# Scales of the first layer spread through DRAM, the halves of q and k exchanged by ScalarE, and fewer transposes in front of two stages

## What is computed

```python
x = x + L0_attn(layernorm(x))           # everything below is L0_attn
x = x + einsum('btd,ed->bte', conv3(x), w_pw)      # three taps over time, then pointwise
q, k, v = split(x @ w_qkv.T)            # 16 heads of 8
q, k = rope(q, sin, cos), rope(k, sin, cos)
q_phi, k_phi = elu(q) + 1, elu(k) + 1
attn = causal_linear_attention(q_phi, k_phi, v) / (denominator + 1e-6)
x = x + sigmoid(delta(x) @ w_gate.T + b_gate) * (attn @ w_o.T)
h = layernorm(x) * ln_g + ln_b
x = x + sum_e softmax(h @ w_moe_gate.T)[e] * (silu(h @ w1[e] + b1[e]) @ w2[e] + b2[e])
```

## Time and profile before

| | us |
|---|---|
| median of three runs | 1480.37 (1479.02 to 1481.9) |
| the profiled execution's own time | 1480.5 |
| its span, first to last instruction | 1478.7 |
| setup, until the second stage starts | 8.1 |
| attention_front | 8.1 to 454.1 |
| mixture | 454.1 to about 896 |
| the three stages behind | about 900 to 1478.7 |

### The profile page before, as it was taken

How to read it: one execution, slowest core, us unless ns; L and a number is a source line. 1 busy time by engine, 2 the same in 40 slices (tenths; PEclk the granted TensorE clock), 3 DMA queues, 4 the chain that set the end, 5 groups by cost and what they waited for, 6 DMA issues and landing times. The chain is left out here.

```text
span 1478.7 us, 33273 instructions
## 1 busy us (share of the span) xinstructions
PE 1266.4 (86%) x10164; PEld 984.0 (67%) x10164; DVE 1013.0 (69%) x3390; ACT 814.8 (55%) x1703; POOL 712.6 (48%) x907
## 2 busy tenths in 40 slices
PE   2899999999986999999999965883988888739998
PEld 1566767676655877777777754773666666539997
DVE  3588888888735899999999984764566666522222
ACT  2355555556426776767777643552556555525554
POOL 3355565656420234343443542335566676426666
PEclk9799999999877999999999986996999999859999
DMA  1101011110102321212112205674111112168872
GB/s 62 40 30 39 31 33 33 31 37 28 45 13 62 69 54 44 64 41 62 40 48 59 73 16 142 196 202 146 27 44 47 49 55 44 44 233 300 266 264 69
DMA packets 70844, 117.53 MB, mean 79 GB/s; under 512 B 9746, under 2 KB 36635, under 8 KB 70768
## 3 DMA queue, kind: packets, MB, share of 16 engines
q1 hardware_dynamic: 58736, 93.49, 21.3%
q0 software_dynamic: 9856, 21.52, 4.6%
q10 hardware_dynamic: 2176, 1.61, 0.4%
HBM read 79.35 MB, written 29.88 MB: 74 GB/s over the span
## 5 line engine op out<-in xcount | busy, mean ns | idle before, releaser
L1159 DVE TENSOR_TENSOR m_Sl<-m_S,m_Sh 128x512 fp32r<-128x512 f32 x256 | 195.5, 769 | 23.3 <-ACT m_S L1076 20.6
L1076 ACT ACTIVATE m_S<-PS,W 128x512 f32<-128x512 f32 x256 | 174.7, 690 | 39.0 <-issue 33.1
L1071 ACT ACTIVATE m_Sh<-PS,W 128x512 fp32r<-128x512 f32 x192 | 132.9, 692 | 72.1 <-PE PS L996 64.5
L1459 POOL DMA_INDIRECT rows<-r_row,r_posi x128 | 131.2, 1025 | 36.2 <-issue 36.0
L761 DVE TENSOR_TENSOR am<-PS,C 128x512 f32<-128x512 f32 x192 | 119.6, 678 | 25.9 <-PE PS L454 25.4
L1693 PEld LDWEIGHTS PS<-f_wt,f_hid 128*128 128x128 f32 x960 | 121.3, 194 | 4.4
L1693 PE MATMUL PS<-f_wt,f_hid 128*128 128x128 f32 x960 | 121.5, 277 | 0.0
L1682 PE MATMUL PS<-f_xT,f_wt 128*128 128x256 f32 x480 | 121.2, 390 | 0.0
L965 POOL TENSOR_TENSOR m_oe<-m_oe 128x512 f32<-128x512 f32 x48 | 67.8, 1412 | 102.2 <-DVE m_oe L1140 101.7
L994 PE MATMUL PS<-m_HH,m_w1h 128*128 128x512 f32 x256 | 107.7, 421 | 7.1 <-DVE m_w1l L1112 4.7
L352 POOL TENSOR_TENSOR am<-am,C 128x512 f32<-128x512 f32 x64 | 81.6, 1275 | 54.8 <-ACT am L636 53.5
(11 more groups left out here) (237 smaller groups left out, 3127.2 us busy)
## 6 DMA issues: line engine op xcount, KB each, us to landing
f_wt<-wr SPq DMA_DIRECT2D x40, 578.0 KB
f_row<-rows SPq DMA_DIRECT2D x40, 260.0 KB
f_wt<-wr SPq DMA_DIRECT2D x40, 256.0 KB, 2.8
m_gb<-gates SPq DMA_DIRECT2D x8, 1024.0 KB, 7.7
m_raw<-gates SPq DMA_DIRECT2D x8, 1024.0 KB, 7.9
f_row<-rows SPq DMA_DIRECT2D x40, 132.0 KB, 2.1
mid<-f_res SPq DMA_DIRECT2D x20, 256.0 KB, 3.3
X<-x SPq DMA_DIRECT2D x16, 256.0 KB, 2.8
```

What stands on the lines that cost most here:

```text
L1071: nc.scalar.activation(Sh[:, n % 4, :], PS[:, n % 3, :], ACT.Silu, bias=w("b1")[:, n:n + 1]).then_inc(sh_ready, 1)
L1076: nc.scalar.activation(S[:, n % 3, :], PS[:, n % 3, :], ACT.Silu, bias=w("b1")[:, n:n + 1]).then_inc(s_ready, 1)
L1159: nc.vector.tensor_tensor(Sl[:, n % 4, :], S[:, n % 3, :], Sh[:, n % 4, :].bitcast(F32), ALU.subtract).then_inc(sl_ready, 1)
L1459: nc.gpsimd.indirect_dma_start(out=self.rows, out_offset=bass.IndirectOffsetOnAxis(ap=self.posi[:, u, t:t + 1], axis=0), in_=self.row[:, u ...
```

## The change

- **Setup merged**: the stage `setup` is gone. Its loads and its VectorE work (`prepare`) are part of `attention_front`; SP loads x of batch 0 first of all, ScalarE's queue loads the weights, and the memset of `vm` on GpSimd comes after the first batch's scaling.
- **x comes in twice**: as tokens (into H, which is free then, for the statistics) and transposed (`xt`, an input laid out on the host: into X and, for the current batch, into `xnT`). X now holds x with features on the partitions during the front and most of the mixture. The mean is taken out by the weights (`centre`: the taps and router 0 are multiplied by I - 1/128 once). The reciprocal deviations go to DRAM and come back broadcast to all partitions (`spread_rstd`, SP), and GpSimd multiplies `xnT` by them (`scale_x`). `normalise`, `turn_xn` and `copy_xnT` are gone.
- **Denominators**: one transpose of `den` (`turn_den`), a small copy, a DMA to DRAM and a broadcast back on ScalarE's queue, in place of `spread_out`, four transposes and `copy_rdT`.
- **Second layer norm**: scale and shift go through DRAM in the same way; GpSimd does `scale_z` and `shift_z` one step later (a fifth batch e = c-1 in the pipeline); `turn_z` and `normalise2` are left for the last batch only.
- **Rotation**: ScalarE copies each half across (`swap_halves`, two instructions for q and two for k), VectorE multiplies by the sines in one operation of 128 partitions.
- **Copies**: `keep_x1` goes from GpSimd to ScalarE; ScalarE also copies x2 (`keep_x2`). `residual2` adds x2T to X from SBUF.
- **mixture**: `ROUNDED = ()`, so ScalarE makes every `Sh`. GpSimd adds X's columns to the total (`sums`, one more large addition and one small one per batch), the transposed total is the new x, ScalarE copies it into X (`copy_back`), the scores come from the total's columns right behind `back` (`pe_scores_columns`) and are multiplied by the reciprocal deviation afterwards. `residual`, `pe_turn` and the copy of xT are gone for layer 0.

The core of the diff:

```diff
@@ attention_front, SP @@
+                sp.dma_start(columns(H, b).rearrange("p (c d) -> p c d", c=CT), src).then_inc(x_in, 16)
+                sp.dma_start(columns(XT, b), xt[:, bass.ds(b * SEQ, SEQ)]).then_inc(xt_in, 16)
+            def load_rows(b):
+                after_previous(sp, pw_psum, b)
+                sp.dma_start(xnT[:, 2:], xt[:, bass.ds(b * SEQ, SEQ)]).then_inc(xnT_in, 16)
+            def spread_rstd(b):
+                sp.wait_ge(rstd1_ready, b + 1)
+                after_previous(sp, rb_in, b, 16)
+                sp.dma_start(rstd_dram.rearrange("(p t) -> p t", p=P), rstd[:, :]).then_inc(rstd_out, 16)
+                sp.wait_ge(rstd_out, 16 * b + 16)
+                after_previous(sp, xn_ready, b)
+                sp.dma_start(rb[:, :], rstd_dram.unsqueeze(0).to_broadcast([P, SEQ])).then_inc(rb_in, 16)
@@ GpSimd @@
+            def scale_x(b):
+                pool.wait_ge(rb_in, 16 * b + 16)
+                pool.wait_ge(xnT_in, 16 * b + 16)
+                nc.gpsimd.tensor_tensor(xnT[:, 2:], xnT[:, 2:], rb[:, :], ALU.mult).then_inc(xn_ready, 1)
+            def scale_z(b):
+                pool.wait_ge(x2_copied, b + 1)
+                pool.wait_ge(sb2_in, 16 * b + 16)
+                nc.gpsimd.tensor_tensor(x2c[:, :], x2c[:, :], sb2[:, 0, :], ALU.mult).then_inc(scaled, 1)
+            def shift_z(b):
+                pool.wait_ge(scaled, b + 1)
+                nc.gpsimd.tensor_tensor(x2c[:, :], x2c[:, :], sb2[:, 1, :], ALU.add).then_inc(z_ready, 1)
...
                 if b is not None:
                     mask_last(b, 0)
-                    keep_x1(b, u)
+                if e_ is not None:
+                    scale_z(e_)
+                if n is not None:
+                    scale_x(n)
...
+                if b is not None:
                     mask_last(b, 1)
+                if e_ is not None:
+                    shift_z(e_)
@@ TensorE @@
-                if n is not None:
-                    turn_xn(n)
                 if c_ is not None:
                     turn_x2(c_)
                 if b is not None:
                     update_state(b, u, 1)
+                    turn_den(b)
                     weigh(b, u, 1)
...
-                if c_ is not None:
-                    turn_z(c_)
                 if n is not None:
                     project(n, u, "q", 0)
-                if c_ is not None:
-                    logits(c_)
+                if e_ is not None:
+                    logits(e_, c_)
...
                 if b is not None:
                     weigh(b, u, 3)
-                    turn_spread(b)
@@ ScalarE @@
+            def swap_halves(b, n):
+                act.wait_ge(qk_psum, 2 * b + n + 1)
+                after_previous(act, phi_ready, b, 2)
+                for o in range(2):
+                    at, to = slice(64 * o, 64 * o + 64), slice(64 - 64 * o, 128 - 64 * o)
+                    ins = nc.scalar.activation(rot[to, n, 1, :], PS[at, 1 - n, :], ACT.Copy)
+                ins.then_inc(swapped, 1)
...
+                if f is not None:
+                    swap_halves(f, 1)
                 if b is not None:
                     copy_k(b)
...
                 if b is not None:
                     raw_scores(b, 1)
+                    keep_x1(b, u)
+                    copy_den(b)
+                    spread_den_out(b)
+                if e_ is not None:
+                    scale_h(e_)
+                if c_ is not None and not final(c_):
+                    keep_x2(c_)
                 if b is not None:
                     raw_scores(b, 2)
+                    spread_den_in(b)
+                if c_ is not None and not final(c_):
+                    spread_scale2_out(c_)
                 if n is not None:
                     copy_x1(n, u)
+                if c_ is not None and not final(c_):
+                    spread_scale2_in(c_)
                 if b is not None:
                     raw_scores(b, 3)
+                if n is not None:
+                    swap_halves(n, 0)
+                if e_ is not None:
+                    copy_logits(e_, c_)
@@ VectorE @@
-                dve.wait_ge(qk_psum, 2 * b + n + 1)
+                dve.wait_ge(swapped, 2 * b + n + 1)
                 nc.vector.tensor_tensor(rot[:, n, 0, :], PS[:, 1 - n, :], c("cos"), ALU.mult)
-                for o in range(2):
-                    at, to = slice(64 * o, 64 * o + 64), slice(64 - 64 * o, 128 - 64 * o)
-                    ins = nc.vector.tensor_tensor(rot[to, n, 1, :], PS[at, 1 - n, :], c("sin")[at], ALU.mult)
-                ins.then_inc(qk_read, 1)
+                nc.vector.tensor_tensor(rot[:, n, 1, :], rot[:, n, 1, :], c("sin"), ALU.mult).then_inc(qk_read, 1)
...
+                nc.vector.tensor_tensor(columns(XT, b), columns(XT, b), x2T[:, :], ALU.add).then_inc(x_added, 1)
@@ mixture @@
-        ROUNDED = (3,)
+        ROUNDED = ()
...
+                if e == 1:
+                    pool.wait_ge(oe_ready, MOE * b + 1)
+                    nc.gpsimd.tensor_tensor(carrier[:, :], minus_half[:, :], minus_half[:, :], ALU.mult).then_inc(carried, 1)
+                    nc.gpsimd.tensor_tensor(acc, acc, XT[:, bass.ds(b * SEQ, SEQ)], ALU.add).then_inc(with_x, 1)
+                    pool.wait_ge(with_x, b + 1)
...
                 mm.then_inc(back_psum, 1)
+                routing.pe_scores_columns(pe, b, oe[:, total_of(v), :])
...
-                    if n == 0:
-                        route(routing.pe_turn, pe, r, v, tr)
-                    if n == 3:
-                        route(routing.pe_scores, pe, r, v, tr)
...
+                    if n == 8 and p is not None:
+                        copy_back(p)
...
-                    if n == 8 and p is not None:
-                        residual(p)
```

378 lines of the change are left out of this document (208 added, 170 removed).

## The result

The changed kernel takes 1505.19 us (median of four runs, 1498.92 to 1511.71), the kernel before beside it 1481.13: ratio 1.016, 95% interval 1.011 to 1.022. It is slower by some 24 us; the prediction was 1454, with 1434 to 1479 as its range, and 0.13 on slower. The profiled execution took 1498.92, its span is 1497.1, 18.4 more than before. It is the shortest of the four, so the trace holds 18 of the 24 us.

What follows compares the result with a forecast made beforehand. In front and mixture TensorE was taken as close to full with VectorE close behind. 1480.5 - 4 (start) + 1.4 (front) - 21 + 1 (mixture) - 3.8 (end) = 1454 us, range 1434 to 1479.

Steps and rivals of the forecast that it cites:

- The start: Before the front: x loaded first and memset later, against a centring matmul and two DMA trips; -4 us, bounds -6 and 0.
- The front: Attention front: TensorE's savings offset by VectorE's waits for GpSimd; step 24.0, +0.1, about 14 steps, +1.4 us in all.
- TensorE waits there in place of the transposes: Front, before the second tile's scores: VectorE's later masks delay them 0.9 us, replacing the first 0.9 of TensorE's saving.
- so that 0.65 becomes idle time: Front: z's transposes, 0.65 us per step, stood where the next projection waits for VectorE's mask anyway, so not counted as gain.
- a further width of either sign: TensorE's granted clock, mean 0.96: less TensorE work may make low-clock stretches longer or fewer; no size given.
- Rival (a): Front: GpSimd's shared port decides, VectorE's five SBUF-only operations each wait 0.45 longer; step 26.2, 1485 us; chance 0.14.
- Rival (d): Front: ScalarE waits for a DRAM store with the last tile's raw scores behind; 1 us per step, 1468; chance 0.12.
- Rival (b): Front: waits for GpSimd fall into VectorE's gaps; step near 22.8, 1437 us; chance 0.2.
- The mixture: TensorE's transposes and VectorE's roundings and residual addition removed; -1.6 us per batch, -21 over 13, first batch +1.
- The end: End of mixture: VectorE's idle 3.77 us before the last batch's scores disappears; -3.8 us.

Runs made afterwards that it cites:

- e11: Changed kernel with GpSimd's three new front operations (scaling of x, scaling and shift of z) cut to 8 of 512 columns; 1468.90 us, 0.995 of the kernel before.
- e2: Changed kernel with four unused transposes of the identity ahead of the state update of tile 1; 1472.11 us, 0.998 of the kernel before.
- e16: Changed kernel with only the older batch's logits moved ahead of the projection of q; 1443.21 us, 0.996 of the kernel before.
- e13: Kernel before with three unused VectorE multiplications, all ahead of the denominators; 1553.78 us, 1.054 of the kernel before.
- e14: Kernel before with three unused VectorE multiplications, spread over three gaps of VectorE; 1474.62 us, 1.001 of the kernel before.
- e5: e2 with ScalarE's load of z's scales issued behind the last tile's raw scores and the copies of q's halves; 1466.05 us, 0.993 of the kernel before.
- e8: Kernel before with `ROUNDED = ()` alone, so ScalarE makes all high parts in the mixture; 1462.19 us, 0.990 of the kernel before.
- e9: e5 with the older batch's logits issued ahead of the projection of q; 1458.05 us, 0.987 of the kernel before.
- e15: Changed kernel, no filler, with the logits ahead of the projection of q and the load of z's scales later; 1466.45 us, 0.993 of the kernel before.
- e7: Kernel before with four unused transposes as filler behind the denominators of each step; 1470.68 us, 0.997 of the kernel before.
- e10: e9 with GpSimd's addition of x in the mixture moved ahead of its inverse deviation; 1452.15 us, 0.987 of the kernel before.
- e12: Kernel before with ScalarE's copies of the halves (new rotation) and no rounding on VectorE; 1459.84 us, 0.989 of the kernel before.

## Why the prediction was wrong, point by point

**The start** was right: -3.8 measured, -4 predicted; the first pointwise matmul begins at 15.76 instead of 18.91.

**The front** is the step that failed: "I take a step of 24.0, +0.1"; the steady step is 27.3. Its placing of the waits held: they are where it put them, and smaller. `x2T<-x2T,x1c` was to lose 0.5 and lost 0.36; `phi` of k 1.1, and it was 0.90; the sine of k 0.6, and it was 0.30. For the first two the overlap was foreseen within a tenth (0.50 and 1.04 us); but VectorE needs only 0.54 or 0.55 us more once GpSimd's operation has ended, and not the 0.68 that it takes alone, so 0.14 less is lost than the overlap is long. The masks of tile 1 were to begin at 10.9 after the step's start and do at 9.99 (265.91 - 255.92). The scores of tile 2 were to begin "near 13.0" and do at 12.90, but that is luck: the masks were 0.9 early, and the low clock used that up (weighing 1.94 us where it takes 1.08 at the full clock).

The Trainium skill says of the shared port that it is an exclusive lock: an instruction of VectorE with two inputs in SBUF and one of GpSimd that reads SBUF keep each other out, the one that comes second waiting (page "SBUF — State Buffer", section "Who interferes with whom"). These rows agree, and e11 takes the waits away with the GpSimd work. What I had drawn from it for the sine multiplication of q doesn't come: it takes 0.68 at 282.07 while GpSimd's power of four elements runs (281.85 to 282.86); there the measurement decides.

What the sum did not contain is what idle places of TensorE do to its clock. I had written down the idle time itself ("TensorE waits there in place of the transposes", "so that 0.65 becomes idle time"), priced each at its own length, and put the clock in one sentence as "a further width of either sign". The transposes taken out stood in exactly the two places where TensorE would otherwise wait for VectorE. Behind the first, work at the low clock then took 3.8 us longer: 0.9 each for weighing and scores, 2.1 for the pointwise matmuls. 3.4 per steady step against 0.1: some 32 us over the stage. The loss is that of the clock, 4.0 per step by the estimate above; the idle time alone, 1.2 more per step, would not have eaten the 1.8 of work that was taken off. That idle places make this loss is shown from both sides: filled, they give it back (e2 with the first, e16 with the second), and made in the kernel before, they bring it (e13, with e14 as its control).

**Rival (a)** gave the right sign and nearly the size (26.2 per step; 27.3 measured), but by the wrong mechanism. It wanted 0.45 more of waiting in each of VectorE's five operations than was placed, and the waits were smaller than placed; e2 leaves them all and wins 27 us. **Rival (d)** is real, but only once the steps are short: e2 and e5 show it. **Rival (b)**'s 22.8 exist too: the first step, without the scaling of z and without logits, takes 22.45. Two slips of the working change nothing: in the earlier trace rows VectorE goes on at 167.08, 2.9 after the load, and not at 166.8; and (b)'s sum is 1437, while the range calls it 1434.

**The mixture** had the right sign and one of its two mechanisms, and was mis-sized: -1.6 per batch predicted, -0.85 measured in the steady part, and the first three batches together 3.8 slower where I had +1. e8 shows that relieving VectorE of the roundings is all of it (-1.0). The 1.2 us of transposes that TensorE loses, and VectorE's residual addition, bring nothing: TensorE waits for `S` from ScalarE instead (7.4 us in the ten batches). The reliefs of two engines that hand work to each other were added up where only one counts.

**The end** came out at -5.7 against -3.8: VectorE's idle 3.77 us before the last scores is gone, and the other 1.9 are within what this last part varies by (644.8 in e5, 635.8 in e9, with the same code in it), so that this term came out is in part luck.

What stays open: the exact condition on which the clock falls. The low stretches differ in length beside equal idle places (10.2 us in the changed kernel, 3.4 and 10.2 in one execution of e15), waits of 1.6 us for GpSimd's mask leave them short in e9, they come every second step in the kernel before with no wait over 0.2 us, and e7's filler pays a little even there. Nor is it the idle place right there that makes the clock fall: in the changed kernel it falls within the first 0.1 us of it, and in half of e13's steps before it. The runs show that filling or making idle places moves them; they do not give a rule to forecast them by.

The fastest versions are e9 and e10, at 0.987 of the kernel before: the change, with its own work in better order and four transposes of filler. Without filler the best of it is e15 (0.993), and on the kernel before `ROUNDED = ()` alone (e8, 0.990), or with the rotation (e12, 0.989), does as well as all of it within the intervals.

## What to carry to other kernels

Before taking work off a TensorE that is nearly full, ask what it will do in that time. If the answer is "wait for another engine", the work removed is worth nothing, and when the granted clock already dips in the trace it can cost more than the gap is long: here steps 3.4 us longer with two gaps of 0.8. Put work that waits for nothing into those places (the logits: two lines, 2%). And when a change moves several things, look for the one line that brings the gain by itself: here `ROUNDED = ()`, 1%.

## What was not expected of the hardware

- Useless transposes made a kernel faster: 1.9% off where TensorE had idled 0.78 us per step, 0.3% where it had waited 0.2 us at most.
- The same 0.78 us ahead of the same instruction went with 10.2 us at the lower clock in every steady step of one kernel, and with 3.4 us in eight of ten cases (10.2 in two) in another, in which a different gap, some 14 us earlier, had been filled. In the first the clock had fallen within 0.1 us after TensorE began to wait.
- GpSimd waits for VectorE too, which the prediction did not price. Cut to 8 columns, its scaling of z, which starts while VectorE works on SBUF, has a mean of 652 ns; the one of x behind it, in the same form, 239. At full size they took 1725 and 1541, where the shift of z, beside VectorE's masks from PSUM, took 1269.
- An operation of VectorE that waits inside itself for GpSimd ends 0.54 or 0.55 us after it, though it takes 0.68 or 0.69 alone (`x2T<-x2T,x1c` and `phi` of k in the changed kernel,'s `phi` of q in the kernel before).
